# The norm's guard as a maximum over pairs, its Newton step on GpSimd, and new tables of order in a fused Mamba and transformer kernel

## The chip, the cores and the metric

The kernel runs on one core of one Trainium2 chip. The metric is the device time of one execution in microseconds (us). A core has a matrix engine (PE), a vector engine (DVE), a scalar engine for activation functions (ACT), a general engine (POOL, also called GpSimd), and a queue that issues transfers (SP). Each runs its own instructions strictly in the order in which they stand; across engines they meet by semaphores alone.

## The reference

A Mamba block over 4 sequences of 1024 tokens of width 128 comes first, then six layers of a small transformer. The change touches the transformer only. Of a layer, this is what matters:

```python
def l2norm(t):
    return t / jnp.maximum(jnp.linalg.norm(t, axis=-1, keepdims=True), 1e-12)

def attn_layer(x, Wqkv, qs, ksc, Wo):          # 16 heads of 64
    q, k, v = jnp.split(x @ Wqkv, 3, -1)
    q = l2norm(q) * qs
    k = l2norm(k) * ksc
    q = q * cos * scale + rotate_half(q) * sin * scale
    k = k * cos * inv + rotate_half(k) * sin * inv
    out = local_attention(q, k, v)             # windows of 32, each sees itself and the one before
    return out @ Wo

for i in range(DEPTH):                         # 6
    x = attn_layer(shift_tokens(x), Wqkv[i], q_scale[i], k_scale[i], Wo[i]) + x
    x = ffn_layer(shift_tokens(x), ...) + x    # layer norm, a * gelu(gate), hidden 341
```

## The kernel before

The activations stay in SBUF in the transposed layout [128 features, tokens]. The Mamba part ends at about 1233 us of the profile; from there to the end the transformer runs, 6 layers of 32 **tiles** of 128 tokens; 4 tiles make a **chunk** of 512 tokens, on which the feed-forward part works, so there are 192 tiles and 48 chunks. The weights of a layer are loaded and prepared while the layer before still runs.

**One tile.** PE projects the tile to 1024 query numbers (`project0`) and then to 1024 key numbers (`project1`), both into the same two banks of PSUM, `heads_ps`. For each, ACT squares them into `sq` (`square0`, `square1`), DVE sums the squares by head (`squares0`, `squares1`) and multiplies the heads with the cosine and the sine tables (`cosines`, `sines`), and POOL adds the two products (`rotated`). PE may overwrite `heads_ps` with the next projection only when DVE has done `cosines` and `sines` of the last. When both sums stand, DVE puts a floor of 1e-24 under the 32 sums (`guard`), ACT makes a first 1/sqrt by Ln and Exp (`inverse_norm`), a Newton step of four small DVE instructions sharpens it (`refine`, L1079 to L1085), and POOL multiplies queries and keys with it (`normed0`, `normed1`). PE turns them (`head_turn0` to `head_turn3`), ACT copies them out (`copy_heads`), PE scores (`score`), DVE finds the maxima (`find_max`), ACT takes exponents (`exponent`, 16 instructions), DVE sums and inverts (`sum_probs`, `invert_sum`), POOL scales (`normalise_probs`), DVE turns (`turn_probs`), PE mixes (`mix`, four windows in four banks), ACT copies four times (`copy_mixed`), PE multiplies with the folded product of value and output weights (`output`), DVE adds to the residual (`add_output`).

**One chunk.** PE `mean`, DVE `centre`, ACT `square`, PE `variance`, ACT `log` and `rstd`, POOL `scale`, ACT `affine` and `round_high`, POOL `rest_high`, PE `gate0` to `gate2` and `value0` to `value2`, ACT `gelu`, DVE `product`, PE `ff_output`, DVE `add_ff`.

**The order** is written out in four tables: `PE_ORDER`, `ACT_ORDER`, `DVE_ORDER` and `POOL_ORDER` each list one cycle of an engine, the work of one chunk, as (lag, tile of the chunk, stage); `sequence` repeats the list, once for each chunk and a few times more to start and end, taking chunk i - lag in turn i. Nothing else sets it. In steady state the kernel is therefore one cycle, repeated; its length is what each chunk costs.

**Four turn banks** of PSUM go round among all of PE's results other than projections and scores, in the order in which PE makes them (`turn_banks`): each use waits until the reader of the use four places earlier has read.

**At a layer's boundary** ACT and POOL prepare the next layer's projection weights: `high_qk` (ACT), `low_qk` (L1205) and `rope` (L1219, L1222, L1225, both POOL), put behind `rotated0` and `rotated1` of the last tile; `project` of the first tile waits for `low_qk`. Two `fold`s per layer multiply value and output weights on PE behind `mean` (L761), each in two turn banks, and ACT copies them (`copy_folded`, L924).

**Tables of ACT.** Gelu needs another table than Exp and Ln. The one is loaded before the first Gelu of a chunk (the load at L1031), and `act.preload_act_table_set` behind the last loads the other (L1034).

Lines which the argument speaks of: L779 `project`, L790 `head_turn`, L801 `row_turn`, L811 and L826 `score`, L838 `mix`, L849 `output`, L856 `mean`, L942 `square`, L964 `copy_heads`, L971 `copy_rows`, L1065 `squares`, L1073 `guard`, L1099 `sines`, L1112 `cosines`, L1125 `sum_probs`, L1130 `invert_sum`, L1153 `centre`, L1238 `rest`, L1245 `rotated`, L1255 `normed`.

## Time and profile before

| what | us |
|---|---|
| median of 3 runs | 4357.74 (4356.62 to 4362.51) |
| the profiled execution | 4357.31 |
| its span, first to last instruction | 4355.4 |
| PE busy in the span | 3877.6 (89%) |
| DVE busy | 3686.1 (85%) |
| ACT busy | 3040.8 (70%) |
| POOL busy | 2855.2 (66%) |

The profiled execution's own time is 1.9 us more than its span. The shares are means over two programs with different limits, the Mamba part and the transformer, so they are read by stretches of the transformer: one cycle in the middle of a layer, and the cycles around a boundary.

### The profile page before, as it was taken

To read this page: it belongs to the slowest core of one execution; us is meant where nothing else is said; L and a number is where in the kernel's file an instruction comes from. 1 tells how busy PE (TensorE), PEld (TensorE's weight loads), DVE (VectorE), ACT (ScalarE), POOL (GpSimd) and SP (SyncE) were. 2 spreads that over 40 slices of the span, in tenths; PEclk is the share of its full clock that TensorE was granted. 3 is DMA by queue.
4 is the path that set the end of the run, shared out by engine and by line. 5 is a ranking of instruction groups with operands and counts; after the bars stand their busy time and mean duration, and the time that the engine had idled before them with its cause. 6 is when DMAs were issued, how large, how long until landed. Compare 5 with 4: busy or idle time off the path is not lost.

```text
span 4355.4 us, 110202 instructions
## 1 busy us (share of the span) xinstructions
PE 3877.6 (89%) x43616; PEld 2575.4 (59%) x43616; DVE 3686.1 (85%) x4248; ACT 3040.8 (70%) x6957; POOL 2855.2 (66%) x1562
## 2 busy tenths in 40 slices
PE   5788888888857999899989999999999999899997
PEld 2333333333326777677767777677766777677775
DVE  3888888888958898899988998888988988888885
ACT  4655564556326887788778887778877778778775
POOL 0555555555637776777777777777776777777773
PEclk8889898898879999999999999999999999999999
DMA  1000000000010000000000000000000000000001
GB/s 39 0 0 0 1 0 0 1 0 0 0 47 5 12 14 2 2 15 2 14 2 5 12 2 14 2 15 2 14 2 5 12 2 14 2 5 2 2 2 40
DMA packets 12011, 34.46 MB, mean 8 GB/s; under 512 B 2404, under 2 KB 4328, under 8 KB 10608
## 3 DMA queue, kind: packets, MB, share of 16 engines
q1 hardware_dynamic: 11504, 27.41, 1.8%
q8 instruction: 353, 5.78, 0.5%
q14 instruction: 154, 1.26, 0.1%
HBM read 23.21 MB, written 4.19 MB: 6 GB/s over the span
## 4 chain that ended last, share of the span: by engine, by line
PE 47%; DVE 14%; ACT 4%; issue 4%; POOL 0%; DVEq 0%; ACTq 0%; POOLq 0%
PE ps L849 12%; PE ps L779 9%; PE ps L838 7%; PE ps L790 6%; PE ps L826 5%; PE ps L887 3%; DVE resid L1112 3%; DVE sq L1099 3%; DVE ssq L1065 2%; PE ps L874 2%; DVE stat L1125 1%; ACT L1034 1%; DVE prob_t L1137 1%; PE ps L811 1%; ACT prob L980 1%
## 5 line engine op out<-in xcount | busy, mean ns | idle before, releaser
L425 POOL TENSOR_TENSOR read<-state,c_row 128x1024 f32<-128x1024 f32 x256 | 598.4, 2356 | 622.1 <-DVE state L411 494.9
L1255 POOL TENSOR_TENSOR resid<-resid,rnorm 128x1024 f32<-128x1024 f32 x384 | 726.8, 1903 | 319.8 <-DVE rnorm L1085 319.8
L1245 POOL TENSOR_TENSOR resid<-resid,sq 128x1024 f32<-128x1024 f32 x384 | 909.4, 2373 | 14.7 <-DVE sq L1099 8.0
L849 PE MATMUL ps<-mixed,w_vo 128*128 128x128 f32 x6144 | 720.5, 276 | 0.4 <-ACT mixed L989 0.4
L849 PEld LDWEIGHTS ps<-mixed,w_vo 128*128 128x128 f32 x6144 | 709.0, 192 | 13.4 <-issue 0.9
L779 PE MATMUL ps<-w_qk,xs_parts 128*128 128x512 f32 x2304 | 643.6, 416 | 55.0 <-DVE resid L1112 27.4
L980 ACT ACTIVATE prob<-ps,stat 128x64 f32<-128x64 f32 x3072 | 648.7, 369 | 0.6 <-DVE stat L1119 0.6
L229 PE MATMUL mamba_ps<-read,ident 128*128 128x512 f32 x1024 | 569.0, 694 | 22.4 <-DVE xc L366 19.8
L942 ACT ACTIVATE sq<-ps 128x1024 f32<-128x1024 f32 x384 | 402.0, 1047 | 232.4 <-PE ps L779 224.9
L779 PEld LDWEIGHTS ps<-w_qk,xs_parts 128*128 128x128 f32 x2304 | 419.6, 194 | 225.0 <-issue 135.9
L1262 POOL TENSOR_TENSOR prob<-prob,stat 128x1024 f32<-128x1024 f32 x192 | 365.4, 1903 | 272.8 <-DVE stat L1130 272.8
L989 ACT COPY mixed<-ps 128x512 f32<-128x512 f32 x768 | 403.0, 629 | 151.4 <-PE ps L838 151.2
L1112 DVE TENSOR_TENSOR resid<-ps,rope_l 128x1024 f32<-128x1024 f32 x384 | 467.1, 1216 | 45.4 <-ACT sq L942 40.6
L790 PE MATMUL ps<-ident,resid 128*128 128x128 f32 x3072 | 446.6, 276 | 54.9 <-ACT rows L971 36.0
L1099 DVE TENSOR_TENSOR sq<-ps,rope_l 128x1024 f32<-128x1024 f32 x384 | 466.8, 1216 | 31.7 <-ACT sq L942 29.0
L838 PE MATMUL ps<-prob_t,rows 32*128 32x512 f32 x3072 | 404.6, 635 | 76.4 <-ACT w_vo L924 36.2
L1065 DVE TENSOR_REDUCE ssq<-sq 128x16 f32<-128x1024 f32 x384 | 464.4, 1209 | 0.0
L790 PEld LDWEIGHTS ps<-ident,resid 128*128 128x128 f32 x3072 | 358.4, 141 | 153.2 <-issue 76.9
L229 PEld LDWEIGHTS mamba_ps<-read,ident 128*128 128x128 f32 x1024 | 207.9, 216 | 309.7 <-issue 259.9
L964 ACT COPY k_t<-ps 128x512 f32<-128x512 f32 x384 | 227.5, 610 | 168.5 <-PE ps L790 168.5
L316 ACT COPY c_row<-mamba_ps 128x1024 f32<-128x1024 f32 x128 | 128.3, 1003 | 270.6 <-PE mamba_ps L209 270.6
L826 PE MATMUL ps<-k_t,q_t 64*32 64x64 f32 (+1 forms) x24576 | 289.2, 225 | 18.1 <-issue 18.1
(139 smaller groups left out, 6285.0 us busy)
## 6 DMA issues: line engine op xcount, KB each, us to landing
w_stage<-w_qk_hbm SPq DMA_DIRECT2D x6, 1024.0 KB, 4.9
vo_stage<-w_v_hbm SPq DMA_DIRECT2D x6, 512.0 KB, 3.6
vo_stage<-w_o_hbm SPq DMA_DIRECT2D x6, 512.0 KB, 4.6
xn<-x_hbm SPq DMA_DIRECT2D x4, 512.0 KB, 5.3
kept<-resid SPq DMA_DIRECT2D x8, 256.0 KB, 3.2
resid<-kept SPq DMA_DIRECT2D x8, 256.0 KB, 4.5
out_hbm<-resid SPq DMA_DIRECT2D x8, 256.0 KB, 2.0
...
```

Source lines behind the costliest of these rows:

```text
L229: last = pe.matmul(y_ps[h][:, c, :], ident[:, :], read[:, (2 * g + h) % 4, c * BANK:(c + 1) * BANK], start=n == 0, stop=n == D_STATE - 1)
L425: pool.tensor_tensor(read[:, u % 4, :], state[:, u % 4, :], c_row[:, (u // 2) % 2, :], ALU.mult).then_inc(read_ready, 1)
L779: last = pe.matmul(ps[:, A + c, :], xs_parts[:, odd, xpart, :], w_qk[:, wpart, cols], start=k == 0, stop=k == 2)
L790: last = pe.transpose(bank[:, j * P:(j + 1) * P], qk[:, tile % 2, col:col + P], ident[:, :])
L838: last = pe.matmul(banks[w], rows[rows_w, tile % 2, own, :], prob_t[rows_w, tile % 2, :, own, :], start=own == 0, stop=own == 1)
L849: last = pe.matmul(bank[:, 0:P], w_vo[:, l % 2, head_at(place_h), :], mixed[:, odd, place_h, :], start=place_h == 0, stop=place_h == HEADS ...
L980: last = act.activation(prob[:, tile % 2, place_h, :], score_ps[:, place_h, :], ACT.Exp, bias=stat[:, tile % 2, 0, place_h:place_h + 1])
L1065: dve.tensor_reduce(ssq[:, tile % 2, part * HEADS:(part + 1) * HEADS], sq[:, 0, :].rearrange("p (h d) -> p h d", d=HEAD_DIM), AX_X, ALU.ad ...
L1099: dve.tensor_tensor(sq[:, 1 + part, :].rearrange("p (h s d) -> p h s d", s=2, d=HEAD_DIM // 2), swapped, table(part, 1, tile).rearrange("p ...
L1112: dve.tensor_tensor(qk[:, tile % 2, part * INNER:(part + 1) * INNER].rearrange("p (h d) -> p h d", d=HEAD_DIM), heads_ps.rearrange("p (h d ...
L1245: pool.tensor_tensor(qk[:, tile % 2, cols], qk[:, tile % 2, cols], sq[:, 1 + part, :], ALU.add).then_inc(done[f"rotated{part}"], 1)
L1255: pool.tensor_tensor(heads, heads, norms, ALU.mult).then_inc(done[f"normed{part}"], 1)
```

## The change

Four things are changed.

1. The Newton step `refine` goes from DVE to POOL, word for word, and reads the floored sums from a buffer of its own.
2. `guard` was a DVE maximum of two tensors (the sums, and the floor broadcast). Now the sums stand in pairs, sum and floor side by side (`ssq` has a last dimension of 2, its second column set once to the floor), and `guard` is a DVE reduction by maximum over the pairs, into `floored`. `squares` waits for `guard` of the tile two back instead of `refine`, and `guard` for that `refine`.
3. The load of the Exp and Ln table is put behind a Gelu whose next user of a table is not a Gelu, instead of behind `gelu2`. In the new order that is `gelu2` again, once in each cycle; behind the very last chunk there is none.
4. The four tables of order are new, and the folded weights are copied ahead of another stage (`FOLD_COPIED_AT`).

```diff
-LAST_GELU = 2
-FOLD_AFTER, FOLD_COPIED_AT = "mean", ("copy_mixed0", 4)
+TABLE_STAGES = ("inverse_norm", "exponent", "log", "rstd", "gelu0", "gelu1", "gelu2")
+FOLD_AFTER, FOLD_COPIED_AT = "mean", ("round", 10)
...
 DVE_ORDER = [
-    (1, 3, "refine"), (3, None, "product0"), (0, 0, "sines0"), (0, 0, "cosines0"), (0, 0, "squares0"),
...
+    (3, 3, "add_output"), (4, None, "product0"), (4, None, "product2"), (3, None, "centre"), (1, 0, "squares1"),
+    (1, 0, "cosines1"), (2, 1, "sum_probs"), (1, 0, "guard"), (2, 1, "invert_sum"), (1, 0, "sines1"), (2, 2, "find_max"),
...
-    ssq = sb("ssq", [P, 2, 2 * HEADS])
+    ssq = sb("ssq", [P, 2, 2 * HEADS, 2])
+    floored = sb("floored", [P, 2, 2 * HEADS])
...
-                act.activation(rnorm[:, odd, :], ssq[:, odd, :], ACT.Ln, scale=float(2 ** NORM_SHIFT)).then_inc(rs_log, 1)
+                act.activation(rnorm[:, odd, :], floored[:, odd, :], ACT.Ln, scale=float(2 ** NORM_SHIFT)).then_inc(rs_log, 1)
...
-                    if k == LAST_GELU:
-                        act.preload_act_table_set("natural_log_exp_and_others")
...
+                tables = [x[0] for x in ACT_SEQ[i + 1:] if x[0] in TABLE_STAGES]
+                if name.startswith("gelu") and tables and not tables[0].startswith("gelu"):
+                    act.preload_act_table_set("natural_log_exp_and_others")
...
-                        after(dve, ("refine", tile - 2))
-                    dve.tensor_reduce(ssq[:, tile % 2, part * HEADS:(part + 1) * HEADS],
+                        after(dve, ("guard", tile - 2))
+                    dve.tensor_reduce(ssq[:, tile % 2, part * HEADS:(part + 1) * HEADS, 0],
...
-                dve.tensor_tensor(s, s, norm_floor[:, 0:1].to_broadcast([P, 2 * HEADS]), ALU.max).then_inc(done["guard"], 1)
-
-            def refine(tile):
-
-                after(dve, ("inverse_norm", tile))
-                r, step = rnorm[:, tile % 2, :], newton[:, :]
-                dve.tensor_tensor(step, ssq[:, tile % 2, :], r, ALU.mult).then_inc(newton_step, 1)
...
+                if tile >= 2:
+                    after(dve, ("refine", tile - 2))
+                dve.tensor_reduce(floored[:, tile % 2, :], ssq[:, tile % 2, :, :], AX_X, ALU.max).then_inc(done["guard"], 1)
...
+            def refine(tile):
+
+                after(pool, ("inverse_norm", tile))
+                r, step = rnorm[:, tile % 2, :], newton[:, :]
+                pool.tensor_tensor(step, floored[:, tile % 2, :], r, ALU.mult).then_inc(newton_step, 1)
+                pool.wait_ge(newton_step, 3 * tile + 1)
+                pool.tensor_tensor(step, step, r, ALU.mult).then_inc(newton_step, 1)
+                pool.wait_ge(newton_step, 3 * tile + 2)
+                pool.tensor_tensor(step, three_halves[:, 0:1].to_broadcast([P, 2 * HEADS]), step, ALU.subtract).then_inc(newton_step, 1)
+                pool.wait_ge(newton_step, 3 * tile + 3)
+                pool.tensor_tensor(r, r, step, ALU.mult).then_inc(done["refine"], 1)
```

What the tables move is seen where the built programs stand side by side. Names in the rows are out<-in with the partitions and elements of the output; behind `waits` stand the stages waited for. Line numbers behind L1070 or so differ between the two programs.

**PE behind `mean`, in the middle of a layer.** Before:

```order
L856 MATMUL ps<-xb,ones_mean 128x512 [waits copy_heads3,add_output]
L838 MATMUL ps<-prob_t,rows 128x512 [waits copy_heads2,copy_heads1,copy_heads0,centre,copy_rows,turn_probs]
L838 MATMUL ps<-prob_t,rows 128x512 x7
L779 MATMUL ps<-w_qk,xs_parts 128x512 [waits sines0,cosines0,rest]
L779 MATMUL ps<-w_qk,xs_parts 128x512 x5
L874 MATMUL ps<-ff_parts,w_parts 128x512 [waits copy_mixed0,rest_high]
```

After:

```order
L856 MATMUL ps<-xb,ones_mean 128x512 [waits add_output]
L790 MATMUL ps<-ident,resid 128x128 [waits copy_heads3,normed0]
L790 MATMUL ps<-ident,resid 128x128 x3
L790 MATMUL ps<-ident,resid 128x128 [waits product0,normed1]
L790 MATMUL ps<-ident,resid 128x128 x3
L790 MATMUL ps<-ident,resid 128x128 [waits product2,normed0]
L790 MATMUL ps<-ident,resid 128x128 x3
L790 MATMUL ps<-ident,resid 128x128 [waits centre,normed1]
L790 MATMUL ps<-ident,resid 128x128 x3
L790 MATMUL ps<-ident,resid 128x128 [waits copy_heads1,normed1]
L790 MATMUL ps<-ident,resid 128x128 x3
L811 MATMUL ps<-sight_hidden,sight_rows 128x512 [waits copy_heads3,copy_heads2,exponent,copy_heads1,copy_heads0]
```

Before, `mix` (L838) came right behind `mean` (L856) and needed the bank that `centre` reads. Now five `head_turn`s and `score` stand between; the bank that `centre` reads goes to the fourth of the turns.

**DVE from `centre` on, in the middle of a layer.** Before (L1153 is `centre`, L1073 and L1079 to L1085 stand in every tile):

```order
L1153 TENSOR_TENSOR xc_ff<-xb,ps 128x512 [waits rest_high,mean]
L1099 TENSOR_TENSOR sq<-ps,rope_l 128x1024 [waits rotated0,square0]
L1112 TENSOR_TENSOR resid<-ps,rope_l 128x1024 [waits head_turn1,head_turn0,square0]
L1079 TENSOR_TENSOR newton<-ssq,rnorm 128x32 [waits inverse_norm]
L1081 TENSOR_TENSOR newton<-newton,rnorm 128x32 [waits newton_step]
L1083 TENSOR_TENSOR newton<-three_halves,newton 128x32 [waits newton_step]
L1085 TENSOR_TENSOR rnorm<-rnorm,newton 128x32 [waits newton_step]
L1065 TENSOR_REDUCE ssq<-sq 128x16 [waits refine,square0]
```

After (`centre` is L1143, `squares` L1066, `cosines` L1102, `sum_probs` L1115, `guard` L1075, `sines` L1089):

```order
L1143 TENSOR_TENSOR xc_ff<-xb,ps 128x512 [waits rest_high,mean]
L1066 TENSOR_REDUCE ssq<-sq 128x16 [waits guard,square1]
L1102 TENSOR_TENSOR resid<-ps,rope_l 128x1024 [waits head_turn3,head_turn2,square1]
L1115 TENSOR_REDUCE stat<-prob 128x16 [waits normalise_probs,exponent]
L1075 TENSOR_REDUCE floored<-ssq 128x32 [waits refine,squares1,squares0]
L1120 RECIPROCAL stat<-stat 128x16 [waits sum_probs]
L1089 TENSOR_TENSOR sq<-ps,rope_l 128x1024 [waits rotated1,square1]
L1109 TENSOR_REDUCE stat<-ps 128x16 [waits score]
```

The four rows of `newton` and `rnorm` are gone, `guard` is a reduction, and `sines1`, for which PE's next `project0` waits, is the sixth instruction behind `centre`.

**POOL around `refine`, in the middle of a layer, after** (before, no row of `newton` stood on POOL; L1235 is `rotated`, L1257 `normed`, L1264 `normalise_probs`):

```order
L1272 TENSOR_TENSOR ff_parts<-xc_ff,ff_parts 128x512 [waits round_high]
L1235 TENSOR_TENSOR resid<-resid,sq 128x1024 [waits sines1,cosines1]
L1243 TENSOR_TENSOR newton<-floored,rnorm 128x32 [waits inverse_norm]
L1245 TENSOR_TENSOR newton<-newton,rnorm 128x32 [waits newton_step]
L1247 TENSOR_TENSOR newton<-three_halves,newton 128x32 [waits newton_step]
L1249 TENSOR_TENSOR rnorm<-rnorm,newton 128x32 [waits newton_step]
L1257 TENSOR_TENSOR resid<-resid,rnorm 128x1024 [waits refine,rotated0]
L1257 TENSOR_TENSOR resid<-resid,rnorm 128x1024 [waits refine,rotated1]
```

The four small instructions stand right ahead of the `normed` that needs them, each waiting for the one before.

**PE at the first fold of a layer.** Before:

```order
L856 MATMUL ps<-xb,ones_mean 128x512 [waits copy_heads3,add_output]
L761 MATMUL ps<-vo_stage 128x128 [waits copy_heads2,copy_heads0,wvo_loaded]
L761 MATMUL ps<-vo_stage 128x128 x7
L838 MATMUL ps<-prob_t,rows 128x512 [waits centre,vo_copied,copy_heads1,copy_rows,turn_probs]
L838 MATMUL ps<-prob_t,rows 128x512 x7
L779 MATMUL ps<-w_qk,xs_parts 128x512 [waits sines0,cosines0,rest]
```

After:

```order
L856 MATMUL ps<-xb,ones_mean 128x512 [waits add_output]
L761 MATMUL ps<-vo_stage 128x128 [waits product0,copy_heads3,wvo_loaded]
L761 MATMUL ps<-vo_stage 128x128 x7
L790 MATMUL ps<-ident,resid 128x128 [waits product2,normed0]
L790 MATMUL ps<-ident,resid 128x128 x3
L790 MATMUL ps<-ident,resid 128x128 [waits centre,normed1]
L790 MATMUL ps<-ident,resid 128x128 x3
L790 MATMUL ps<-ident,resid 128x128 [waits vo_copied,normed0]
L790 MATMUL ps<-ident,resid 128x128 x3
L790 MATMUL ps<-ident,resid 128x128 [waits vo_copied,normed1]
```

Before, `mix` waited for the copies of the fold. Now the third and the fourth `head_turn` behind the fold wait for them (`vo_copied`). On ACT the two copies (L924) stood behind `exponent` and `square` of the chunk; now they stand behind two `copy_heads`.

## Rows read from the trace of the kernel before

**Rows 1.** The page's busy time of each engine, its first line of part 1.

```profile
PE 3877.6 (89%) x43616; PEld 2575.4 (59%) x43616; DVE 3686.1 (85%) x4248; ACT 3040.8 (70%) x6957; POOL 2855.2 (66%) x1562
```

**Rows 2.** Stretches: one steady cycle, then the two cycles around a boundary.

```profile
core 0: us, PE busy (x) PEld busy (x) DVE busy (x) ACT busy (x) POOL busy (x), PEclk, DMA share, GB/s
2500.53:2560.39 59.86, 57.93 (x860) 44.25 (x861) 54.41 (x75) 48.49 (x131) 45.56 (x27) 1.00 0.01 2
2209.60:2283.00 73.40, 62.22 (x877) 47.30 (x876) 61.03 (x75) 51.49 (x135) 56.15 (x35) 0.95 0.01 2
2283.00:2348.60 65.60, 60.86 (x877) 45.88 (x876) 54.40 (x75) 50.07 (x134) 45.00 (x27) 0.97 0.01 2
```

**Rows 3.** Waits of the steady cycle, PE's: total us, times, longest.

```profile
PE ps L838 <- DVE xc_ff L1153: 0.9, 1, 0.9
PE ps L790 <- ACT rows L971: 0.8, 1, 0.8
```

**Rows 4.** Chain of waits, the steady cycle's: start, us, engine, line.

```profile
2517.80 0.44 PE ps L790 x4
...
2526.26 0.32 PE ps L811 x2
2526.58 1.41 PE ps L826 x91
...
2529.91 0.70 DVE xc_ff L1153
2530.75 2.00 PE ps L838 x16
...
2558.09 1.15 ACT L1034
```

**Rows 5.** Groups by line in the steady cycle: count | busy us, mean ns.

```profile
L1245 POOL TENSOR_TENSOR resid<-resid,sq 128x1024 f32<-128x1024 f32 x9 | 21.3, 2371 | 0.0
...
L1065 DVE TENSOR_REDUCE ssq<-sq 128x16 f32<-128x1024 f32 x8 | 9.7, 1210 | 0.0
...
L1079 DVE TENSOR_TENSOR newton<-ssq,rnorm 128x32 f32<-128x32 f32 x4 | 2.3, 568 | 0.1
...
L1238 POOL TENSOR_TENSOR xs_parts<-xa,xs_parts 128x128 fp32r<-128x128 f32 x4 | 1.8, 456 | 0.7 <-ACT xs_parts L933 0.7
L1073 DVE TENSOR_TENSOR ssq<-ssq,norm_floor 128x32 f32<-128x32 f32 x4 | 1.8, 443 | 0.4
...
L1130 DVE RECIPROCAL stat<-stat 128x16 f32<-128x16 f32 x4 | 1.0, 250 | 0.1
...
L1081 DVE TENSOR_TENSOR newton<-newton,rnorm 128x32 f32<-128x32 f32 x4 | 0.8, 192 | 0.1
```

**Rows 6.** Groups by line from 2000 to 4000 us.

```profile
L924 ACT COPY w_vo<-ps 128x512 f32<-128x512 f32 x16 | 9.7, 731 | 0.0
...
L1222 POOL TENSOR_TENSOR rope_l<-rope,head_scale 128x512 f32<-128x512 f32 x8 | 10.3, 1282 | 0.0
...
L1219 POOL TENSOR_TENSOR partner_scale<-head_scale,partner_sign 128x64 f32<-128x64 f32 x8 | 2.6, 330 | 0.0
```

**Rows 7.** Timeline of DVE and POOL ahead of a boundary: start, us, engine, line.

```profile
2252.04 2.35 POOL L1205 TENSOR_TENSOR w_qk<-w_stage,w_qk 128x1024 fp32r<-128x1024 f32 x1
2252.17 2.27 DVE L1081 TENSOR_TENSOR newton<-newton,rnorm 128x32 f32<-128x32 f32 x1
...
2257.09 1.90 POOL L1255 TENSOR_TENSOR resid<-resid,rnorm 128x1024 f32<-128x1024 f32 x1
2257.12 1.23 DVE L1112 TENSOR_TENSOR resid<-ps,rope_l 128x1024 f32<-128x1024 f32 x1
```

**Rows 8.** PE's waits from 2215 to 2420 us, around a boundary.

```profile
PE ps L838 <- ACT w_vo L924: 7.2, 2, 3.6
PE ps L779 <- DVE resid L1112: 3.5, 1, 3.5
PE ps L790 <- POOL resid L1255: 3.3, 1, 3.3
```

48 lines of the change are left out of this document (18 added, 30 removed), and 42 rows, old and new, of tables (ACT_ORDER, DVE_ORDER, PE_ORDER, POOL_ORDER).

## The prediction

> **What bounds the kernel now.** The page's busy times come first [rows 1]: PE is the busiest engine with 89%, but that is a mean over the Mamba part and the transformer. The stretches [rows 2] are read next. One steady cycle, the work of one chunk, takes 59.86 us, and PE is busy for 57.93 of them; DVE follows with 54.41, ACT with 48.49, POOL with 45.56. So PE paces the transformer, and an ideal order could take no more than 59.86 - 57.93 = 1.93 us off a cycle. PE's waits say what these 1.93 us are [rows 3]: 0.9 us in which `mix` waits for the bank that `centre` reads, 0.8 us in which a `head_turn` waits for `copy_rows`, and some 0.2 us of issue. The chain [rows 4] shows where both stand. `mix` starts at 2530.75, behind `centre` (2529.91, 0.70 us), which waited for the `mean` right ahead of `mix`. The `head_turn` is late because the load of the Exp and Ln table (from 2558.09, 1.15 us of it on the chain) stands ahead of `copy_rows`. DVE is dense: what it does late is done late on ACT and POOL. The third view is a boundary. The cycle with the first fold and the new weights takes 73.40 us, the next 65.60 [rows 2]: 13.5 and 5.7 us over a steady one, 19 us a layer, five times. PE's waits there [rows 8] are 3.6 us for the copies of each fold, 3.5 us of `project` on `cosines`, 3.3 us of `head_turn` on `normed`. The clock of PE falls to 0.95 and 0.97 in those cycles and stands at 1.00 in the steady one.
>
> **What the change costs and gives, part by part.**
>
> *Refine off DVE.* Four instructions a tile. The first took 568 ns in the mean, the second 192 [rows 5], the other two as much as the second. So 4 x (0.57 + 3 x 0.19) = 4.6 us a cycle leave DVE. The 0.57 is no work: an instruction of that size takes 0.19 and the rest is a stall. How the stall comes about is seen ahead of a boundary [rows 7]: the second one took 2.27 us, and ended just when POOL's 2.35 us of `low_qk` ended. DVE's `cosines`, which reads PSUM and SBUF, took 1.23 us beside a POOL instruction that started with it, no longer than the 1.21 us of a sum over as many numbers [rows 5]. So a DVE instruction whose two inputs both lie in SBUF stands behind POOL's, and the others don't. After the change no DVE instruction of the cycle has two SBUF inputs.
>
> *Guard.* It took 443 ns [rows 5], for the same reason. The reduction over pairs reads 64 numbers a partition from one SBUF input. No such row exists. Bounds: an instruction of that kind and size from above, the inversion of 16 numbers, 0.25 us, and from below zero gain, 0.44. I take 0.25, nearest in size and in having one input. That gives back 0.8 us a cycle, and DVE comes down to 54.4 - 4.6 - 0.8 = 49.0 us of 58 or so.
>
> The Trainium skill (Perfetto Trace Analysis, section Optimizing Scalar/DVE Operations) speaks against the move: since GpSimd and DVE share an SBUF read port, moving work between those two might not help. Another of its pages (SBUF — State Buffer, section SBUF: two separate sides) calls the pair an exclusive lock, which a DVE instruction with two SBUF inputs contends for. By the second, the move helps more than its 0.19 us instructions would; by the first, not at all, and that is the rival "nothing gained" below.
>
> *Refine on POOL.* 4 x 4 instructions of 32 elements. The trace has no such row. Nearest are 330 ns for 64 elements [rows 6] and 456 ns for 128 [rows 5]. The line through both gives 0.27 us for 32. Each waits for the one before it; DVE's own hop was 0.03 us (0.1 us of idle ahead of four [rows 5]), and 0.15 is an upper estimate, from the hop of DVE to PE at `mix` (2529.91 + 0.70 to 2530.75 [rows 4]). From 4 x 0.2 = 0.8 to 4 x 0.33 + 3 x 0.15 = 1.8 us a tile; I take 1.2. POOL goes from 45.6 to 50.4 us a cycle (52.8 at the upper bound), still 5 to 7 us below PE. What hides it is this slack. It would be exposed only where `normed` is needed at once. In the new order `normed` is finished several us before the `head_turn` that reads it, on my walk below.
>
> *The tables of order.* I walked one cycle of the new tables with the durations of the trace, PE's stages laid end to end, and looked at each wait for whether its producer can be done. All but one have 0.4 us or more to spare. The 0.9 us at `mean` goes: behind `mean` now come five `head_turn`s and `score`, and the bank of `centre` is needed by the fourth turn, 3 x 0.44 = 1.3 us behind `mean`, when `centre` (0.70) is done. The 0.8 us at `copy_rows` goes too: behind `gate2` stand `value1`, two `head_turn`s and a `project` before the next user of its bank. The one tight place is new. Behind `centre` DVE has squares1, cosines1, sum_probs, guard, invert_sum and sines1, in this row, and PE's next `project0` waits for the last. Instructions of this size follow each other at 1.13 us (rows say 1.21 each, of which the next overlaps 0.08) [rows 5]: 0.70 + 4 x 1.14 + 2 x 0.27 + 0.1 = 5.9 us behind `mean`. PE has until then 5 x 0.44 + 0.32 + 1.41 + 2.00 = 5.9 us of work [rows 4]. So a wait of 0 to 0.5 us; I take 0.25.
>
> Steady cycle after: 57.93 + 0.2 (issue) + 0.25 = 58.4 us, 1.47 less. Of the 47 intervals between the 48 chunks all profit, fill and end of the pipeline aside, which hold the same stages: 47 x 1.47 = 69 us.
>
> *The table load.* One per cycle before and after, behind the same Gelu, and none behind the last chunk (1.3 us of ACT, when nothing waits). Nothing.
>
> *Folds.* Before, the copies (0.73 us each [rows 6]) began only behind `exponent`, and PE stood 3.6 us. Now, counted from the end of `mean`: fold 1.0, first turn 0.45, then on ACT two `copy_heads` and the first copy of the fold, a bank each and so at most 0.73 us each: 1.5 + 3 x 0.73 = 3.7 us. The third turn could start at 1.9. So 1.8 us of wait at most, then little more. Saved: 1.8 us, twice a layer, and of the slow clock (PE was busy 60.86 us in a cycle with nothing more than a fold of 1.2 us over 57.93 [rows 2]) perhaps 0.5 each.
>
> *Boundary on POOL.* Behind `rotated0` of the last tile POOL has low_qk0 (2.35), rope0 (0.33 + 2 x 1.28), normalise_probs (1.9), rotated1 (2.37), low_qk1 (2.35) before PE may start `project1` of the new layer: 11.9 us. `rotated0` can start when `cosines0` and `sines0` of its tile are done, by the walk 12.8 us ahead of that `project1`, and then ends 10.4 ahead: PE would stand 1.5 us. But POOL is by the walk still in `normed` of the tile before for 3.2 us, and so PE stands 4.7. Behind it come rope1 (2.9), refine (1.2) and normed0 (1.9), then `head_turn1`: another 2 us or so, and 1 in small waits. That is 7.7 us against 3.5 + 3.3 = 6.8 before. A loss of 0.9, and 1.4 for the clock, which falls behind a long wait. Refine lies here on the path: 1.2 us of the loss are its.
>
> By layer 2 x (1.8 + 0.5) - 2.3 = 2.3 us saved, five times 12 us.
>
> **Sum.** 69 + 12 = 81 us off the profiled execution, 4357.3, which is the median within 0.4 us. 4357.3 - 81 = 4276 us.
>
> **Rivals.** (1) *The walk is too kind*: half of the 1.47 us is lost in a new wait, since a walk with mean durations sees no chance delays, and DVE's row of six behind `centre` has no reserve. Against it stand DVE's 5 us of new slack. 47 x 0.7 + 5 = 38 us: 4319. (2) *All of it*: the cycle comes to 58.0 and the boundaries give 5 us each, since DVE no longer stands 4 to 5 us there in Newton steps behind low_qk and rope: 47 x 1.9 + 25 = 114: 4243. (3) *Nothing gained*: POOL's added work delays DVE as much as it is relieved, through the port. Against it is `cosines` in rows 7. 4355. (4) *Slower: POOL takes the pace.* POOL is in order, and each of its 16 new instructions may cost more than the line says. It would have to take 58.4 - 45.6 = 12.8 us a cycle, 0.8 us each, for POOL to be as busy as PE, and 0.9 for the cycle of before; at 1.0 us each the cycle is 61.6 and the kernel 4357 + 47 x 1.7 + 5 x 3 = 4450. Or, less: refine holds `normed` up at 0.6 us each, and a wait of more than 1.5 us a cycle comes with it: 47 x 0.5 + 5 x 2 = 33 us over, 4390. For it speaks only that the price at 32 elements is not shown; against it, 0.33 us at 64. (5) *The change doesn't do what it says*: the load of the table could stand elsewhere. It doesn't; the rows of the order show it behind `gelu2`.
>
> **How the numbers follow.** A difference under 0.2% (9 us) can't be told from none here. My forecast has 0.55, the kind walk's failure 0.17, all of it 0.16, nothing 0.05, slower 0.07. Faster: 0.88, same 0.05, slower 0.07. The range for 8 in 10 takes in the second rival's 4243 and most of the first: 4243 to 4332.
>
> **What would show it.** A cycle of 58.2 to 58.6 us, PE busy 57.9 of it. DVE at 49 us a cycle, its instructions on 64 numbers at 0.25, with no long ones. POOL at 50.4, its small ones at 0.27. PE's wait for `centre` gone, a short one of `project` (L779) on `sines` in its place. At a fold 1 to 2 us instead of 3.6; at a boundary one wait of `project` of 4 to 5 us. I am wrong if POOL's Newton instructions take over 0.6 us, if the cycle is still 59 or more, or if the boundary's two cycles exceed a steady pair by more than 19 us.

## The result: 4175.3 us, twice the gain that was forecast

| | before | after |
|---|---|---|
| median of 4 runs, us | 4360.12 (4356.62 to 4366.58) | 4175.32 (4174.16 to 4178.99) |
| span of the profiled execution | 4355.4 | 4176.9 |
| mean granted clock of PE | 0.948 | 0.952 |

The ratio of the times is 0.9576, with a 95% interval of 0.9559 to 0.9593: 185 us less. The forecast was 81 us less, 4276 us, with a range from 4243 to 4332. The sign was right and the size too small by a factor of 2.3. Every median here and below is over a kernel's fast runs; one slow run of e3, at 14864.14 us, is left out.

The page after, the first line of part 1 (busy time of each engine) answers to [rows 1], and the first line of part 4 gives the shares of the chain that ended last:

```profile
PE 3828.7 (92%) x43616; PEld 2570.0 (62%) x43616; DVE 3409.8 (82%) x3480; ACT 3048.1 (73%) x6956; POOL 3035.9 (73%) x2330
...
PE 64%; issue 2%; ACT 1%; POOL 1%; DVE 0%; POOLq 0%; ACTq 0%; DVEq 0%
```

The same part 4 of the kernel before:

```profile
PE 47%; DVE 14%; ACT 4%; issue 4%; POOL 0%; DVEq 0%; ACTq 0%; POOLq 0%
```

DVE lost 276 us of busy time and POOL got 181. The chain of before ran through DVE for 14% of the span; after, it hardly touches DVE. PE has the same 43616 matmuls in both, and yet is busy for 49 us less.

Stretches of the kernel after (columns as in [rows 2]): two plain cycles, then the two around a boundary:

```profile
core 0: us, PE busy (x) PEld busy (x) DVE busy (x) ACT busy (x) POOL busy (x), PEclk, DMA share, GB/s
2401.81:2459.76 57.95, 57.47 (x862) 44.47 (x861) 49.44 (x58) 48.92 (x130) 49.35 (x42) 1.00 0.01 2
3880.56:3937.70 57.14, 57.12 (x864) 44.33 (x860) 49.38 (x59) 48.77 (x130) 49.26 (x43) 1.00 0.01 2
2156.30:2224.40 68.10, 62.17 (x881) 47.22 (x880) 50.58 (x62) 52.64 (x135) 57.23 (x50) 0.96 0.01 2
2224.40:2284.50 60.10, 58.77 (x874) 45.13 (x874) 49.03 (x56) 48.76 (x131) 51.41 (x44) 0.99 0.01 2
```

In the two plain cycles PE is busy for all but 0.48 and 0.02 us. The second takes 57.14 us, less than the 57.93 us for which PE was *busy* in the cycle of [rows 2]. So the floor of the prediction was no floor.

PE's waits from 1500 to 4100 us (engine, line waited for: total us, times, longest), before and then after:

```profile
PE ps L838 <- ACT w_vo L924: 36.2, 10, 3.6
PE ps L790 <- ACT rows L971: 32.9, 42, 1.1
PE ps L838 <- DVE xc_ff L1153: 27.0, 31, 0.9
PE ps L790 <- POOL resid L1255: 15.8, 5, 3.3
PE ps L779 <- DVE resid L1112: 12.9, 5, 3.5
```

```profile
PE ps L779 <- issue: 18.2, 7, 3.6
PE ps L790 <- ACT w_vo L924: 13.1, 10, 1.3
PE ps L826 <- issue: 8.5, 19, 1.8
```

The waits on DVE and on `copy_rows` are gone. What is left sits mostly at boundaries: `project` (L779, its five long ones are the first `project1` of a new layer, which by the order of the program waits for POOL's `low_qk1`), and the fold. A wait put down to "issue" is one whose releaser the records don't name.

**Where the 178.5 us of span went.** I split each transformer at the starts of its 48 `centre` instructions, one per chunk, as the timeline lists them: 35 plain intervals, 10 around the five boundaries, the last two, and ahead of the first the filling of the pipeline, from the first fold on PE. The sums are my own arithmetic from those rows and from PE's busy time in each interval; the columns for three experiments are used below.

| us | before | after | e1: new code, old order | e2: new order, Newton on DVE | e12: fastest |
|---|---|---|---|---|---|
| 35 plain intervals | 2123.9 | 2016.8 | 2106.1 | 2053.7 | 2014.2 |
| PE busy in them | 2035.9 | 2005.8 | 2025.1 | 2022.6 | 2005.3 |
| PE idle in them | 88.1 | 11.0 | 81.0 | 31.1 | 8.9 |
| their median (shortest) | 60.34 (59.86) | 57.54 (57.19) | 60.06 (59.54) | 58.54 (58.32) | 57.49 (57.19) |
| 10 boundary intervals | 692.2 | 637.1 | 691.4 | 637.0 | 620.2 |
| fill | 137.1 | 120.8 | 135.3 | 127.4 | 120.7 |
| last two | 99.0 | 100.2 | 98.9 | 101.4 | 101.7 |

After against before: 107 us in the plain cycles, 55 at the boundaries, 16 in the fill, and the last two cost 1. Of the 107, 77 are idle time of PE (2.52 us a cycle before, 0.31 after) and 30 are busy time for the same matmuls (58.17 us a cycle before, 57.31 after).

### The profile page after: what moved, and what is told of

It reads as the page before. It is cut to its first block, busy times and chain, and to the rows that moved or that the text cites. A ratio compares the mean times of both kernels' runs of the same rounds, so it can differ in the third digit from the quotient of the medians.

```text
span 4176.9 us, 110200 instructions
## 1 busy us (share of the span) xinstructions
PE 3828.7 (92%) x43616; PEld 2570.0 (62%) x43616; DVE 3409.8 (82%) x3480; ACT 3048.1 (73%) x6956; POOL 3035.9 (73%) x2330
## 4 chain that ended last, share of the span: by engine, by line
PE 64%; issue 2%; ACT 1%; POOL 1%; DVE 0%; POOLq 0%; ACTq 0%; DVEq 0%
PE ps L849 16%; PE ps L779 12%; PE ps L838 9%; PE ps L790 8%; PE ps L826 6%; PE ps L874 5%; PE ps L887 3%; PE ps L811 1%; PE ps L801 1%; PE ps L856 1%; PE ps L862 1%; ACT prob L980 0%; PE ps L761 0%; ACT mixed L989 0%; POOL resid L1257 0%
## 5 line engine op out<-in xcount | busy, mean ns | idle before, releaser
L1235 POOL TENSOR_TENSOR resid<-resid,sq 128x1024 f32<-128x1024 f32 x384 | 909.8, 2375 | 4.0 <-DVE sq L1089 3.7
L1257 POOL TENSOR_TENSOR resid<-resid,rnorm 128x1024 f32<-128x1024 f32 x384 | 725.5, 1905 | 17.8
L849 PEld LDWEIGHTS ps<-mixed,w_vo 128*128 128x128 f32 x6144 | 709.6, 192 | 12.9 <-issue 4.6
L779 PE MATMUL ps<-w_qk,xs_parts 128*128 128x512 f32 x2304 | 641.3, 414 | 47.3 <-issue 18.2
L1089 DVE TENSOR_TENSOR sq<-ps,rope_l 128x1024 f32<-128x1024 f32 x384 | 462.7, 1205 | 119.1 <-ACT sq L942 118.8
L1102 DVE TENSOR_TENSOR resid<-ps,rope_l 128x1024 f32<-128x1024 f32 x384 | 464.5, 1210 | 74.6 <-ACT sq L942 67.5
L779 PEld LDWEIGHTS ps<-w_qk,xs_parts 128*128 128x128 f32 x2304 | 414.8, 192 | 164.0 <-issue 81.1
L1264 POOL TENSOR_TENSOR prob<-prob,stat 128x1024 f32<-128x1024 f32 x192 | 366.2, 1907 | 174.9 <-DVE stat L1120 174.8
L1066 DVE TENSOR_REDUCE ssq<-sq 128x16 f32<-128x1024 f32 x384 | 465.7, 1213 | 8.1 <-ACT sq L942 3.7
L790 PE MATMUL ps<-ident,resid 128*128 128x128 f32 x3072 | 413.9, 274 | 14.3 <-ACT w_vo L924 13.1
L838 PE MATMUL ps<-prob_t,rows 32*128 32x512 f32 x3072 | 383.8, 613 | 4.2 <-DVE xb L1137 1.6
L964 ACT COPY q_t<-ps 128x512 f32<-128x512 f32 x384 | 230.4, 600 | 124.0 <-PE ps L790 121.7
```

The lines of the kernel that those rows point to most:

```text
L779: last = pe.matmul(ps[:, A + c, :], xs_parts[:, odd, xpart, :], w_qk[:, wpart, cols], start=k == 0, stop=k == 2)
L790: last = pe.transpose(bank[:, j * P:(j + 1) * P], qk[:, tile % 2, col:col + P], ident[:, :])
L838: last = pe.matmul(banks[w], rows[rows_w, tile % 2, own, :], prob_t[rows_w, tile % 2, :, own, :], start=own == 0, stop=own == 1)
L849: last = pe.matmul(bank[:, 0:P], w_vo[:, l % 2, head_at(place_h), :], mixed[:, odd, place_h, :], start=place_h == 0, stop=place_h == HEADS ...
L1066: dve.tensor_reduce(ssq[:, tile % 2, part * HEADS:(part + 1) * HEADS, 0], sq[:, 0, :].rearrange("p (h d) -> p h d", d=HEAD_DIM), AX_X, ALU ...
L1102: dve.tensor_tensor(qk[:, tile % 2, part * INNER:(part + 1) * INNER].rearrange("p (h d) -> p h d", d=HEAD_DIM), heads_ps.rearrange("p (h d ...
```

## The experiments

All times are medians. What is said to be less or more than before, and each ratio with its 95% interval, is against the kernel before in the same set of runs (4359.4 to 4360.7); what is said against after is against 4175.3. Four questions were asked: which part of the change gives the gain, what the two small moves off DVE's two-input instructions are worth, whether POOL has anything to spare, and what the waits of the old order cost.

**e1: the new code in the old order.** The four tables and the fold's place are those of before; `guard` is the reduction, and `refine` stands on POOL ahead of the first `normed` of its tile.

```
 POOL_ORDER = [
-    ... (2, 3, "rotated1"), (2, 3, "normed1"), ...
+    ... (2, 3, "rotated1"), (2, 3, "refine"), (2, 3, "normed1"), ...
```

> The old four tables of order with the new code: the Newton step on GpSimd, put right ahead of the first normed of its tile and taken out of VectorE's table, the guard as a reduction over pairs, the fold's copies where they were. Theory A (the stalls of VectorE behind GpSimd are what the kernel of before lost): most of the 185 us come, 100 to 160, the cycle falls from 60.3 to 58.5 or less, the waits of project and head_turn at a boundary shrink. Theory B (the order is what counts, the moved code only relieves an engine that was not the bound): 0 to 50 us, the two waits of the steady cycle (0.9 us of mix on centre, 0.8 us of head_turn on copy_rows) stay.

4334.97 us (4332.06 to 4335.1), ratio 0.994 (0.9925 to 0.9955): **26 us** less than before. The code without the new order is 14% of the gain. PE's waits from 1500 to 4100 us are the old ones (the line numbers differ by one):

```profile
PE ps L839 <- ACT w_vo L925: 36.2, 10, 3.6
PE ps L791 <- ACT rows L972: 31.7, 41, 1.1
PE ps L839 <- DVE xc_ff L1144: 27.9, 32, 0.9
PE ps L791 <- POOL resid L1258: 27.6, 10, 4.4
```

DVE's relief left these waits alone: `copy_rows`, the bank of `centre` and the fold hold PE as long as before. 18 of the 26 us come off the plain cycles, 7 of them idle time and 11 busy time of PE. At the boundaries one wait changed its name: there are now 27.6 us for `normed` where before there were 15.8 for it and 12.9 for `cosines`, and the ten boundary intervals are as long as before (691.4 against 692.2).

**e2: the new order with Newton back on DVE.** `guard` stays the reduction; `refine` is put into DVE's table some instructions behind each `guard`.

```
 DVE_ORDER = [
-    ... (2, 2, "find_max"), ...
+    ... (2, 2, "find_max"), (1, 0, "refine"), ...
```

> The new tables of order with the Newton step back on VectorE, set two to four stages behind guard; the guard stays a reduction. Theory A: VectorE's four small instructions stall behind GpSimd as before, 1.3 us a tile and more at a boundary, and the new order has a row of six behind centre without reserve: 4250 to 4330 us. Theory B: nearly the whole gain stays, 4180 to 4220 us, since VectorE has 8 us of slack in a cycle.

4225.85 us, ratio 0.9693 (0.9679 to 0.9707): **135 us** less than before, and **50 more** than after. So the new tables and the fold's place with the new guard give 135 of the 185. The move to POOL is worth 50 us in the new order, while in the old one move and guard together gave 26. The groups between 2500 and 3500 us show the Newton instructions on DVE in e2:

```profile
L1081 DVE TENSOR_TENSOR newton<-floored,rnorm 128x32 f32<-128x32 f32 x67 | 30.8, 460 | 0.0
```

and on POOL in after:

```profile
L1243 POOL TENSOR_TENSOR newton<-floored,rnorm 128x32 f32<-128x32 f32 x67 | 17.0, 254 | 14.5 <-ACT rnorm L952 14.5
```

On DVE the first of the four takes 0.46 us in the mean, where 0.19 is its time without a stall; the other three take 0.30, 0.19 and 0.22. PE's waits in e2 from 1500 to 4100 us have a row that neither kernel has, 15 of the 50 us: `mean` waits for DVE's `add_output`, 40 times. `project` has 7 us more of waits at "issue" (25.2 in 33 places against 18.2 in 7).

```profile
PE ps L856 <- DVE xb L1149: 15.4, 40, 1.4
```

The table above says where the 50 us stand: 37 in the plain cycles and 7 in the fill. The ten boundary intervals are 637.0 against 637.1: there the Newton step on DVE costs nothing.

**e3: only the fold's copies earlier, in the kernel before.**

```
-FOLD_AFTER, FOLD_COPIED_AT = "mean", ("copy_mixed0", 4)
+FOLD_AFTER, FOLD_COPIED_AT = "mean", ("exponent", 6)
```

> The kernel before with one number changed: the copies of the folded weights stand ahead of the exponent of a tile instead of ahead of copy_mixed. The wait of mix for them was 3.6 us, twice a layer. If the fold is an own part of the gain, it is 10 x 2 to 3 us = 20 to 30 us, the slow clock behind the wait with it. If the waits only move (ACT now waits for the fold), within 10 us of before.

4332.3 us (three runs, 4330.09 to 4337.56), ratio 0.9938 (0.9921 to 0.9954): **28 us** less. PE's wait for the copies fell from 36.2 to

```profile
PE ps L838 <- ACT w_vo L924: 13.1, 10, 1.3
```

which is 23.1 us; the ten boundary intervals fell from 692.2 to 669.2, again 23. That the two agree is in part chance: of the 23 us of interval 12 are idle and 11 busy time of PE, since some of the idle time came back in other places (6.8 us in which a feed-forward projection now waits for `copy_mixed`, and 6.7 us more ahead of `score`). So the fold's place is a part of the change by itself, worth 4.6 us a layer, as the prediction had it.

**e4: the guard as a maximum of two tensors again, on DVE, in the kernel after.**

```
-dve.tensor_reduce(floored[:, tile % 2, :], ssq[:, tile % 2, :, :], AX_X, ALU.max)
+dve.tensor_tensor(floored[:, tile % 2, :], ssq[:, tile % 2, :, 0], ssq[:, tile % 2, :, 1], ALU.max)
```

> The kernel after with the guard as a VectorE maximum of two tensors in SBUF instead of a reduction over pairs. The instruction should go from 0.21 us to 0.4 to 0.5 in the mean, with single ones over 1.5, as before. Theory A: it delays inverse_norm and what is queued on VectorE; 10 to 40 us over after. Theory B: no change that can be measured, since TensorE never waits in the cycle.

4220.98 us, ratio 0.9676 (0.966 to 0.9692): **46 us more** than after, for one of the smallest instructions of the kernel. The group of `guard` between 2500 and 3500 us, in e4 and then in after:

```profile
L1075 DVE TENSOR_TENSOR floored<-ssq 128x32 f32<-128x32 f32 x68 | 101.4, 1491 | 3.1
```

```profile
L1075 DVE TENSOR_REDUCE floored<-ssq 128x32 f32<-128x64 f32 x68 | 14.6, 214 | 3.1
```

1.49 us against 0.21 us for the same 32 maxima. It isn't the work: 154 of e4's 192 guards took over 0.6 us, and every one of them ended within 0.25 us behind the end of a POOL instruction. [rows 5] had 0.44 for it in the old order, where 58 of 192 were so long. The Trainium skill (SBUF — State Buffer, section SBUF: two separate sides) says that GpSimd and DVE share a port pair under an exclusive lock, for which a DVE instruction contends if both of its inputs lie in SBUF (or if it runs in a two-port performance mode). The two rows agree, with 1.28 us between them.

Of the 46 us, 32 stand in the plain cycles, 6 in the fill and 2 at the boundaries. A plain cycle is 0.92 us longer: 0.41 us of PE's idle time, 0.51 of its busy time. By the tile of the chunk the guards took 0.94, 1.27, 2.06 and 1.63 us in the mean.

**e7: the same guard, one of the four moved behind `sines1`.** It is the one which stands among the six instructions behind `centre`.

```
-    (1, 0, "cosines1"), (2, 1, "sum_probs"), (1, 0, "guard"), (2, 1, "invert_sum"), (1, 0, "sines1"), ...
+    (1, 0, "cosines1"), (2, 1, "sum_probs"), (2, 1, "invert_sum"), (1, 0, "sines1"), (1, 0, "guard"), ...
```

> The kernel after with the guard as a maximum of two tensors, as in the run that cost 46 us, but set behind sines1 instead of ahead of it in the row that follows centre (one tile of four). If those 46 us came from the guard delaying sines1 and with it TensorE's next project0, most of them go: 4175 to 4190 us. If they came from the guard delaying inverse_norm and normed, they stay: 4215 to 4230.

4239.88 us, ratio 0.9724 (0.9709 to 0.9738): **19 us more** than e4, not less. The timeline of e7 (start, us, engine, line; in square brackets the idle time before it) shows why:

```profile
2917.81 0.18 DVE L1075 TENSOR_TENSOR floored<-ssq 128x32 f32<-128x32 f32 x1
2918.02 0.23 ACT L950 ACTIVATE rnorm<-floored 128x32 f32<-128x32 f32 x1 [2.37 <-DVE floored L1075]
...
2918.68 0.25 POOL L1243 TENSOR_TENSOR newton<-floored,rnorm 128x32 f32<-128x32 f32 x1 [1.72 <-ACT rnorm L952]
...
2919.87 1.90 POOL L1264 TENSOR_TENSOR prob<-prob,stat 128x1024 f32<-128x1024 f32 x1
...
2921.80 1.25 DVE L1127 STREAM_TRANSPOSE prob_t<-prob 128x1024 f32<-128x1024 f32 x1 [2.68 <-POOL prob L1264]
```

The guard itself now took 0.18 us, with POOL idle; over the kernel the moved one fell from 0.94 to 0.34 us in the mean, and none of the 38 guards that met no POOL instruction took longer than 0.18. So two inputs alone, POOL aside, cost nothing. But ACT waited 2.37 us for it, and POOL 1.72 us for ACT; POOL's `normalise_probs` came behind the Newton step, and DVE stood 2.68 us for that. Engines that each follow their own order pass a delay round.

**e5: four more small instructions on POOL in each tile,** behind the Newton step's third, into a buffer that nobody reads.

```
+pool.tensor_tensor(spare[:, :], floored[:, tile % 2, :], three_halves[:, 0:1].to_broadcast([P, 2 * HEADS]), ALU.mult)
+... (four times, each waiting for the one before)
```

> The kernel after with four more small GpSimd instructions in every Newton step (they write a buffer that nothing reads), each waiting for the one before: 1.3 us a tile, 5.3 us a cycle, so GpSimd comes from 49.3 to 54.6 us of 57.2. Theory C (TensorE's own work is the cycle, GpSimd has its slack all through): within 15 us of after, that is under 4190. Theory D (normed and the probabilities are needed nearly as soon as they are done): 47 x 1 to 3 us more, 4230 to 4320.

4222.55 us, ratio 0.9689 (0.9675 to 0.9703): **47 us more** than after, though POOL seemed to have 8 us of slack in a cycle of 57. 26 of them are in the plain cycles and 11 at the boundaries.

**e9: e5, and POOL's `normalise_probs` of one tile ahead of the Newton step that stood before it.**

```
-    (0, 1, "rest"), (0, 2, "rest"), (0, 0, "rotated0"), (0, 0, "refine"), (1, 1, "normalise_probs")]
+    (0, 1, "rest"), (0, 2, "rest"), (0, 0, "rotated0"), (1, 1, "normalise_probs"), (0, 0, "refine")]
```

> The run with four more GpSimd instructions in each Newton step (4222.6 us), with one exchange in GpSimd's table: normalise_probs of the tile before stands ahead of that Newton step instead of behind it. Theory E (one chain of every fourth tile is what costs: squares1, cosines1, sum_probs, guard, inverse_norm, Newton step, normalise_probs, turn_probs, cosines0, sines0, then TensorE's project1): the exchange takes inverse_norm and the Newton step out of it, and the time falls to 4175 to 4190. Theory F (GpSimd's added work costs because GpSimd is then nearly full, 54.6 of 57.2 us): it stays at 4210 or more.

4214.03 us, ratio 0.9667 (0.9651 to 0.9684), 8.5 us less than e5. A plain cycle of it (columns as above):

```profile
2955.60:3013.00 57.40, 56.80 (x860) 44.06 (x856) 48.75 (x59) 47.97 (x130) 52.51 (x58) 1.00 0.01 2
```

POOL is busy for 52.5 of 57.4 us. The place of `normalise_probs` explains 8.5 of the 47 us. The rest comes with POOL still 5 us short of full, so what it has left over is not where it is needed. Whether POOL's sum costs, or that each `normed` is ready 1.3 us later, no run tells apart.

**e10: e4 with the exchange shown at e9. e11: the kernel after with the same exchange.**

> The run with the guard as a maximum of two tensors (4221.0 us) with the same exchange. The guard's stall of 1.3 us then still delays invert_sum and sines1 on VectorE, but inverse_norm and the Newton step, 2 us, are out of the way of normalise_probs. Theory E: 4175 to 4190. Theory F, or if the stall acts through sines1 and project0: 4210 to 4225.

> The kernel after with the exchange alone. TensorE hardly waits in its cycle, so theory E gives little: 4168 to 4178 us, the part of the cycles of 57.5 to 58.3 that stands over 57.2. 20 us or more off would say that the chain costs in the kernel after as well.

e10 4221.7 us, ratio 0.9686 (0.9672 to 0.9701), e11 4175.64, ratio 0.9581 (0.9567 to 0.9596): both the same as without it, within 1 us. So the place of that one `normalise_probs` is not how the two-input guard costs its 46 us.

**e13: e10 with the last guard of a chunk moved behind `cosines0`.**

```
-    ... (1, 3, "squares1"), (1, 3, "guard"), (1, 1, "find_max"), (0, 0, "sines0"), (0, 0, "cosines0"), ...
+    ... (1, 3, "squares1"), (1, 1, "find_max"), (0, 0, "sines0"), (0, 0, "cosines0"), (1, 3, "guard"), ...
```

> The guard as a maximum of two tensors and the exchange on GpSimd (4221.7 us), with one guard of four, that of a chunk's last tile, moved on VectorE from ahead of find_max, sines0 and cosines0 to behind them. In its trace that guard takes 1.74 us where the reduction takes 0.21, and TensorE's project1 waits 0.45 us behind cosines0. Theory G (the guard's cost is this one place, the shortest slot between two projections): the wait goes and 30 us or more come back, 4180 to 4195. If the stalls of the other three guards cost as much: 4210 or more.

4216.95 us, ratio 0.9682 (0.9667 to 0.9696): 5 us less, near nothing. PE's waits from 1500 to 4100 us of e10, and then of e13:

```profile
PE ps L779 <- issue: 31.5, 39, 3.6
```

```profile
PE ps L779 <- issue: 14.7, 6, 3.6
PE ps L790 <- ACT k_t L964: 14.2, 34, 0.4
```

The moved guard fell from 1.62 to 0.46 us in the mean. The move took a wait of 0.4 us from `project` in some 32 cycles, and one of 0.4 us on `copy_heads` came in its place. Here the wait that was removed had another right behind it. The guard with the longest stall, the third of a chunk with 2.06 us, was moved in no run.

**e6: the kernel before with the Newton step left out.** One reduction of `rnorm` into itself stands for its four instructions.

```
-dve.tensor_tensor(step, ssq[:, tile % 2, :], r, ALU.mult).then_inc(newton_step, 1)
... (and the other three instructions of the step)
+dve.tensor_reduce(r, r.unsqueeze(2), AX_X, ALU.max).then_inc(done["refine"], 1)
```

> The kernel before without the Newton step: its four VectorE instructions with two SBUF inputs are replaced by one reduction of one input that changes nothing, so the output lacks the refinement of the inverse norm. VectorE loses 5 us a cycle and all the stalls behind GpSimd but the guard's. If the Newton step on VectorE was what cost time in the old order, 80 us or more come off. If the old order's two fixed waits are what stays (as the run of the old order with the new code says), 15 to 35 us.

4321.87 us, ratio 0.9915 (0.9898 to 0.9931): **38 us** less. To leave the step out altogether gives less in the old order than its mere move gives in the new one, 50 us.

**e14: the kernel before with `copy_rows` ahead of `gelu2`,** and so ahead of the table load which delays it.

```
-    (0, 0, "round"), (3, None, "gelu2"), (1, 1, "copy_heads1"), (1, 0, "copy_rows"), (1, 3, "square0"),
+    (0, 0, "round"), (1, 0, "copy_rows"), (3, None, "gelu2"), (1, 1, "copy_heads1"), (1, 3, "square0"),
```

> The kernel before with one move on ScalarE: copy_rows ahead of gelu2, and so ahead of the load of the Exp and Ln table, instead of behind both. It is one of the two fixed waits of the steady cycle, 0.8 us. If what the waits show is what they cost, 35 to 45 us come off (4315 to 4325). If a wait hides restarts of TensorE besides, more than that. If the next wait stands right behind, under 15 us.

4372.97 us, ratio 1.0037 (1.0023 to 1.0051): **13 us more** than before. The wait of 32.9 us for `copy_rows` is gone from 1500 to 4100 us, and `project`'s wait for `cosines` has grown from 12.9 us in five places to 60.5 in 41:

```profile
PE ps L779 <- DVE resid L1112: 60.5, 41, 2.4
```

The timeline of one such place shows what is behind it:

```profile
2896.58 0.39 ACT L971 COPY rows<-ps 128x256 f32<-128x256 f32 x1
...
2897.37 1.99 DVE L1073 TENSOR_TENSOR ssq<-ssq,norm_floor 128x32 f32<-128x32 f32 x1
...
2899.40 0.23 ACT L950 ACTIVATE rnorm<-ssq 128x32 f32<-128x32 f32 x1 [2.43 <-DVE ssq L1073]
...
2901.42 1.90 POOL L1255 TENSOR_TENSOR resid<-resid,rnorm 128x1024 f32<-128x1024 f32 x1 [2.11 <-DVE rnorm L1085]
...
2904.30 0.93 PE L779 MATMUL ps<-w_qk,xs_parts 128*128 128x512 f32 x3 [1.49 <-DVE resid L1112]
```

The guard started 0.45 us behind POOL's `rotated` (L1245, from 2896.92 for 2.40 us), and ended just behind it, after 1.99 us. Over the kernel the guard of each chunk's last tile went from 0.42 to 1.79 us in the mean, and the other three stayed as they were; the median of all went from 0.38 to 0.78 us. Two gaps of 2.43 and 2.11 us follow on ACT and POOL, and PE gets its `project` 1.49 us late.

**e15: e1, with the earlier fold (as in e3) and the earlier `copy_rows` (as in e14).** All of it in the old order.

```
+FOLD_AFTER, FOLD_COPIED_AT = "mean", ("exponent", 6)
...
-    (0, 0, "round"), (3, None, "gelu2"), (1, 1, "copy_heads1"), (1, 0, "copy_rows"), (1, 3, "square0"),
+    (0, 0, "round"), (1, 0, "copy_rows"), (3, None, "gelu2"), (1, 1, "copy_heads1"), (1, 3, "square0"),
```

> The old tables of order with all that was tried on them at once: the new code (26 us alone), the fold's copies earlier (25 us alone), copy_rows ahead of gelu2 (the run beside this one). If they add up, 4270 to 4290, and the rest down to 4175, some 100 us, is the new tables' alone: the other fixed wait, at centre, and the boundaries.

4277.58 us, ratio 0.9819 (0.9804 to 0.9834): **82 us** less than before. Alone the three are worth 26, 28 and minus 13, in sum 41. If the other two still give their 54, the move that costs 13 us where `guard` can be held up by POOL gives 82 - 54 = 28 where it can't. The cycles bear that out: the 35 plain ones, which the fold's place leaves alone (2122.4 us in e3 against 2123.9), take 2080.3 us in e15 and 2106.1 in e1, 26 us less. e1 with only one of the two wasn't run. PE's waits of e15 from 1500 to 4100 us:

```profile
PE ps L791 <- POOL resid L1258: 41.7, 44, 5.3
PE ps L839 <- DVE xc_ff L1144: 28.8, 33, 0.9
```

The fixed wait on `centre`'s bank stays: this run leaves PE's order as it was. The wait for `copy_rows` is gone, and PE now waits for `normed` instead, 5.3 us at each of the five boundaries and mostly 0.3 us in 39 other places.

**e8: the second `low_qk` right behind the first and its `rope`, in the kernel after,** so that `project1` has its weights earlier.

```
-insert_after(pool, (f"rotated{part}", last), (f"low_qk{part}", l), (f"rope{part}", l))
+insert_after(pool, (f"rotated{part}", last), *([("low_qk0", l), ("rope0", l), ("low_qk1", l)] if part == 0 else [("rope1", l)]))
```

> The kernel after with low_qk1 of the next layer moved on GpSimd from behind rotated1 to behind rope0. The project1 of a new layer waits 3.6 us for it in the kernel after; low_qk1 would be done some 4 us earlier. If that wait is an own cost, 5 x 3 to 5 us with the slow clock behind it: 4150 to 4160 us. If normalise_probs and rotated1, which are now late by 2.4 us, give it back: 4170 or more.

4184.37 us, ratio 0.9599 (0.9584 to 0.9613): **9 us more** than after. `project`'s waits fell from 18.2 to 0.5 us, and the wait has moved to the `head_turn`s, that is to `normed` behind the longer row of POOL:

```profile
PE ps L790 <- POOL resid L1257: 21.2, 5, 4.3
```

**e12: after with the exchange of e11 and still earlier copies of the fold.**

```
-FOLD_AFTER, FOLD_COPIED_AT = "mean", ("round", 10)
+FOLD_AFTER, FOLD_COPIED_AT = "mean", ("copy_heads1", 7)
```

> The exchange, and the copies of the folded weights ahead of copy_heads1 instead of ahead of round. The head_turn behind the fold waits 1.3 us for them in the kernel after, ten times. If the wait goes, 10 to 15 us under the run with the exchange alone; if score is late instead by the two copies, no difference.

**4163.08 us** (4160.45 to 4164.81), ratio 0.955 (0.9536 to 0.9564) against before: the fastest of all, 12.6 us under e11 and 12.2 under the kernel after. The wait of 13.1 us for the copies is gone, and the ten boundary intervals fell from e11's 634.6 to 620.2.

## Why the prediction was wrong

By its own steps, in its order:

*What bounds the kernel.* PE paces it: right, and after the change truer than before. The step "an ideal order could take no more than 59.86 - 57.93 = 1.93 us off a cycle" is **the one that failed first**, in both numbers. The 59.86 was the shortest of the 35 plain intervals; their mean was 2123.9 / 35 = 60.68, of which PE stood idle for 2.52 and not 1.93 us. In the fifth layer stood cycles such as these two (columns as above), PE busy for 59.80 and 58.24 us of them:

```profile
3533.20:3596.70 63.50, 59.80 (x860) 44.96 (x860) 54.36 (x75) 48.70 (x131) 45.53 (x27) 0.97 0.01 2
3471.60:3533.20 61.60, 58.24 (x860) 44.41 (x860) 54.39 (x75) 48.72 (x131) 45.59 (x27) 1.00 0.01 2
```

And 57.93 was no least time of the 860 matmuls. The groups by line in one steady cycle, before and then after, show where most of it lies (count | busy us, mean ns | idle us before them):

```profile
L790 PE MATMUL ps<-ident,resid 128*128 128x128 f32 x64 | 9.2, 275 | 0.8 <-ACT rows L971 0.8
```

```profile
L790 PE MATMUL ps<-ident,resid 128*128 128x128 f32 x64 | 8.5, 273 | 0.0
```

The same 64 turns, each as long as before, cover 9.2 us in a cycle in which PE waits among them, and 8.5 us where it doesn't, laid closer end to end. Why PE's matmuls are spread more in a cycle with waits isn't shown by the records, in which the ends of matmuls are modelled. Three errors of the same sign add up to what is missing. The mean interval became 3.06 us shorter ((2123.9 - 2016.8) / 35) instead of 1.47: 0.82 us more for the cycle chosen (60.68 - 59.86), 0.62 for the busy time (57.93 against a mean of 57.31), and 0.14 for the idle time (0.45 us of issue and new wait in the sum, 0.31 measured).

*Refine off DVE, and the guard.* DVE's busy time came to 49.4 us, forecast 49.0. The new guard took 0.214 us, taken as 0.25. Both right, and so was the reading of [rows 7] that the long ones are stalls. **What failed is the weight given to it**: the sum has no term for DVE's relief, and only rival (2) gives it one, at the boundaries. e2 and e4 measured 50 and 46 us for it in the new order, nearly all in the plain cycles and the fill and at most 2 at the boundaries. With Newton back on DVE (e2) the plain cycle has a median of 58.54 us, near the 58.4 that was forecast for the kernel in which Newton had left it: the forecast cycle was that of the order with DVE's stalls still in it. In the old order move and guard together gave 26. That fits a DVE whose stalls hide where PE waits anyway and become PE's where it doesn't, but no run followed such a stall to PE.

*Refine on POOL.* 254 ns each where 0.27 was taken; the hop between two was 15.1 us over 192, 0.08 us, inside the bounds. POOL's busy time was 49.3 us, forecast 50.4. That the 16 instructions are hidden held so far as PE has no wait for `normed` after the change. But "5 to 7 us below PE" is no measure of the room: e5 put 4 more such instructions in a tile and lost 47 us.

*The tables of order.* Both fixed waits went, as walked. The tight place, `project0` on `sines1`, got no wait at all: taken 0.25. PE's chain in a plain cycle of after goes on from `score` into `mix` and `project` with 0.02 us of idle time (start, us, line):

```profile
3522.66 1.41 PE ps L826 x91
3524.07 0.02 issue
3524.09 2.00 PE ps L838 x16
3526.09 1.59 PE ps L779 x6
```

The measured wait is the lower of the two bounds given, zero.

*The table load.* Nothing, as said: 48 loads of the Exp and Ln table before and 47 after, 1.283 us each.

*Folds.* The wait went from 3.6 to 1.3 us each where at most 1.8 was allowed. e3 has 23 us for ten of them, the 2.3 us each that were forecast. The parts were not the forecast's 1.8 of wait and 0.5 of clock, but 1.2 of idle time and 1.1 of busy time, so the sum was met with some luck. A fold itself took 1.15 us, where the sums have 1.0 in one place and 1.2 in another.

*Boundary on POOL.* The step which puts 7.7 us of waits against 6.8 before, and with the clock a loss of 2.3 us, failed. The row of POOL instructions is as walked, here its end at one boundary:

```profile
2215.40 2.38 POOL L1235 TENSOR_TENSOR resid<-resid,sq 128x1024 f32<-128x1024 f32 x1
...
2217.71 2.36 POOL L1195 TENSOR_TENSOR w_qk<-w_stage,w_qk 128x1024 fp32r<-128x1024 f32 x1
...
2220.18 1.19 PE L779 MATMUL ps<-w_qk,xs_parts 128*128 128x512 f32 x2 [3.60 <-issue]
```

PE stood 3.6 us instead of 4.7, and there was no wait for `normed` behind it, forecast as 2 to 3 us. A boundary gave 11.0 us ((692.2 - 637.1) / 5). 6.1 us are two intervals at the plain gain of 3.06, and 4.9 came beyond, where 2.3 was forecast; that is 13 us over the five.

*The sum.* It had no term for the fill. The filling of the pipeline, 137.1 us before and 120.8 after, gave 16 us more. Why isn't shown, except that 7 of them need Newton on POOL (127.4 in e2).

*The rivals.* "All of it" (4243, chance 0.16) was nearest, but the reason that it gives, DVE's Newton steps at the boundaries, isn't what paid: e2 has them back on DVE and its boundary intervals are as short. It took the same floor, 58.0 us a cycle, and so ended 68 us above the time. "POOL takes the pace" didn't come, though e5 shows that four more small instructions a tile already cost 47 us. "Nothing gained" rested on a rule of the Trainium skill (Perfetto Trace Analysis, section Optimizing Scalar/DVE Operations), by which a move from DVE to GpSimd might not help; e2 measured 50 us for the move, and the measurement decides.

**What stays open.** No run had the new tables with all of the old code, so what the order is worth alone isn't measured; with the new code it and the fold's place are worth 4335.0 - 4175.3 = 160 us (e1 against after). If the 50 of the move (e2) and the 46 of the guard (e4) could be taken off together, the tables and the fold's place would be left with 89, but e14 and e15 show that such parts don't add up. Why the cycles of the last two layers ran at 61 to 63.5 us before isn't shown. Nor is the path by which the two-input guard costs PE 46 us: e7, e10 and e13 each took away one candidate and none gave it back. The old order with only `mean` moved wasn't tried, nor were the four new tables one by one.
